# A fused four-layer kernel: three sequences of the first shared experts are moved from their own stage into the head of the fused loop, and scattered rows get a pitch of 1088 bytes

## What is computed

```
scores = softmax(t @ gate_w.T);  weights, indices = top_k(scores, 2)
for e in range(16):
    y = y + swiglu(t, w1[e], w3[e], w2[e]) * weight_of(e)      # routed
z = swiglu(t, sw1, sw3, sw2)                                     # shared: silu(t@sw1.T) * (t@sw3.T) @ sw2.T
return y + z
```

## Time and profile before

| | |
|---|---|
| three runs, median (lowest to highest) | 1965.39 us (1960.8 to 1970.16) |
| the profiled execution's own time | 1962.86 us |
| its span | 1961.1 us |
| TensorE matmul busy | 1831.5 us (93%) |
| VectorE / ScalarE / GpSimd busy | 1264.7 / 763.2 / 422.5 us |
| VectorE, one product of `up` (line 769), mean | 0.419 us |
| VectorE, one tile normalised (line 685), mean | 0.418 us |
| ScalarE, one Silu (line 644) / one copy of 512 columns (649) | 0.382 / 0.586 us |

### The profile page before, as it was taken

The page is one execution under the profiler, slowest core; times in us unless marked ns, Lnnn a source line. Parts: engine busy times, 40 slices in busy tenths (PEclk is TensorE's granted clock), DMA queues, the critical chain, the costliest instruction groups (busy, mean ns, idle before and its releaser), DMA issues.

```text
span 1961.1 us, 33597 instructions
## 1 busy us (share of the span) xinstructions
PE 1831.5 (93%) x9969; PEld 1414.6 (72%) x9987; DVE 1264.7 (64%) x3621; ACT 763.2 (39%) x1479; POOL 422.5 (22%) x708
## 2 busy tenths in 40 slices
PE   5999999979989999667999999999999999999998
PEld 3566666547776666445888888888888888888886
DVE  3677677527432222368778877887787778777843
ACT  1466666543223333234433343334333333433321
POOL 1244334331763444300100110011001100110000
PEclk9899999879998999867999999999999999999999
DMA  9900000001332333252012202220222022112210
GB/s 359 220 6 1 0 0 1 1 1 38 114 108 84 94 94 93 81 199 81 25 63 87 82 16 76 87 81 6 87 85 63 25 86 81 46 46 71 66 49 11
DMA packets 92119, 137.87 MB, mean 70 GB/s; under 512 B 18548, under 2 KB 76148, under 8 KB 91508
## 3 DMA queue, kind: packets, MB, share of 16 engines
q1 hardware_dynamic: 85108, 117.83, 19.0%
q0 software_dynamic: 6912, 18.92, 2.7%
HBM read 98.51 MB, written 38.22 MB: 70 GB/s over the span
## 4 chain that ended last, share of the span: by engine, by line
PE 45%; issue 38%; DVE 9%; POOL 4%; ACT 2%; DMA 1%; another core or an unknown queue 1%; DVEq 0%; SPq 0%; POOLq 0%; ACTq 0%
PE bank L599 6%; PE bank L184 5%; PE bank L1151 4%; PE bank L620 4%; PE bank L1216 3%; PE bank L1109 2%; PE bank L548 2%; PE bank L193 2%; PE bank L1157 2%; PE bank L1244 2%; PE bank L1139 2%; PE bank L559 1%; PE bank L610 1%; PE bank L1202 1%; PE bank L528 1%
## 5 line engine op out<-in xcount | busy, mean ns | idle before, releaser
L184 PE MATMUL bank<-moe_xT,up_w 128*128 128x256 f32 x2304 | 546.1, 380 | 0.0
L184 PEld LDWEIGHTS bank<-moe_xT,up_w 128*128 128x128 f32 x2304 | 438.7, 191 | 60.0
L227 ACT ACTIVATE moe_silu<-bank 128x256 f32<-128x256 f32 x288 | 110.4, 383 | 575.6 <-PE bank L184 572.4
L193 PE MATMUL bank<-down_w,moe_hT 128*128 128x256 f32 x1152 | 304.0, 387 | 3.5 <-ACT moe_y L230 2.1
L193 PEld LDWEIGHTS bank<-down_w,moe_hT 128*128 128x128 f32 x1152 | 207.1, 190 | 37.0 <-issue 6.4
L1390 DVE TENSOR_REDUCE q_slots<-bank 128x4 f32<-128x1024 f32 (+1 forms) x96 | 117.7, 1226 | 82.2 <-PE bank L1151 81.6
L1298 ACT ACTIVATE probs<-bank 128x1024 f32<-128x1024 f32 x96 | 98.1, 1022 | 100.4 <-PE bank L1157 100.4
L599 PE MATMUL bank<-up_w,moe_xT 128*128 x320 | 116.8, 488 | 0.7 <-ACT moe_xT L663 0.6
L794 DVE TENSOR_TENSOR moe_h<-moe_silu,bank 128x176 f32<-128x176 f32 x80 | 27.0, 338 | 138.8 <-issue 86.4
L1151 PE MATMUL bank<-kT,qT 16*128 16x256 f32 (+1 forms) x1024 | 115.3, 353 | 0.2 <-issue 0.2
L294 DVE TENSOR_TENSOR moe_hT<-moe_silu,bank 128x256 f32<-128x256 f32 x256 | 107.7, 421 | 8.8
(11 more groups left out here) (287 smaller groups left out, 3181.5 us busy)
## 6 DMA issues: line engine op xcount, KB each, us to landing
up_w<-comb_rows SPq DMA_DIRECT2D x32, 768.0 KB, 6.0
m<-decay_rows SPq DMA_DIRECT2D x16, 1024.0 KB, 4.9
comb_got<-results SPq DMA_DIRECT2D x16, 768.0 KB, 7.7
moe_rows<-sorted_in SPq DMA_DIRECT2D x80, 128.5 KB
sorted_in<-zero SPq DMA_DIRECT2D x10, 1024.0 KB, 9.5
down_w<-comb_rows SPq DMA_DIRECT2D x16, 512.0 KB, 8.4
up_w<-in_up SPq DMA_DIRECT2D x2, 3168.0 KB, 15.0
up_w<-in_up SPq DMA_DIRECT2D x2, 2304.0 KB, 11.9
```

The source lines that it names most:

```text
L184: last = mm(k.bank[:, UP_BANK + i % 3, half * S:(half + 1) * S], m.w_up[:, c, at + half * m.inter:at + (half + 1) * m.inter], m.xT[:, par, ...
L193: last = mm(k.bank[:, SUM_BANK, j * D:(j + 1) * D], m.hT[:, i % 3, j * P:(j + 1) * P], m.w_down[:, m.expert(i), :], start=(i == 0 and j == ...
L227: nc.scalar.activation(m.silu[:, i % 3, :], k.bank[:, UP_BANK + i % 3, 0:S], ACT.Silu).then_inc(m.silu_ready, 1)
```

## The change

Sequences 13, 14 and 15 leave the shared stage (`EARLY = 13`): it goes through 13 sequences, and the 32 scatters are spread over the 27 places of sequences 4 to 12. The three are computed by new steps `l_norm`, `l_turn`, `l_up`, `l_h`, `l_down` in the head of the fused loop, in buffers that belong to the fourth sublayer, with all transposes, and the result of `l_down`, in bank 7, and with one store buffer. The step `l_h` is VectorE's product, which stands apart from `l_up` there. `decay_in` stands ahead of `gate` now. `l_end`, after the first period, waits for the last of these. The copy of the places and the spare operation ahead of the indirect DMAs are gone, and the rows in `pairs` and `sorted_in` are 272 floats, 1088 bytes, apart; whole rows of 1088 bytes are scattered and 1028 of them fetched. The weights of the shared experts stay where they are while the fourth sublayer's weights are loaded: these take other columns.

```diff
+LINE = 16
+LINED = -(-ROW // LINE) * LINE
+PAIR_ROWS = 2
+EARLY = 13
 def shared_steps(chunks):
+    places = chunks * (EARLY - SCATTERS_FROM)
-    for t in range(B):
+    for t in range(EARLY):
...
-            if t >= SCATTERS_FROM and tile < TILES:
+            place = chunks * (t - SCATTERS_FROM) + c + 1
+            while place > 0 and tile < -(-TILES * place // places):
                 yield "scatter", tile, 0
                 tile += 1
-    yield "down", B - 1, 0
+    yield "down", EARLY - 1, 0
...
 def sparse_vector(k, m, dve):
+    v.memset(m.pairs[:, :, :, ROW:], 0.0)
...
 def sparse_pool(k, m, pool):
-            chain.link(g.tensor_copy(m.place[:, 2 * par:2 * par + 2], cols(m.places, t, 2)))
-            g.tensor_tensor(k.pool_spare[:, 0:1], k.minus_half[:, 0:1], k.minus_half[:, 0:1], ALU.add)
             for j in range(2):
-                at = bass.IndirectOffsetOnAxis(m.place[:, 2 * par + j:2 * par + j + 1], 0)
-                g.indirect_dma_start(m.sorted_in, at, m.pairs[:, par, j, :], None).then_inc(m.scattered[par], 16)
+                at = bass.IndirectOffsetOnAxis(m.places[:, 2 * t + j:2 * t + j + 1], 0)
+                g.indirect_dma_start(m.sorted_in, at, m.pairs[:, row, j, :], None).then_inc(m.scattered[row], 16)
...
+def late_tensor(k, m, pe):
+        if what == "l_turn":
+            pe.wait_ge(s.xn_ready, t + 1)
+            pe.wait_ge(s.y_read, t)
...
+        if what == "l_up":
+            pe.wait_ge(s.xT_ready, m.turns + n + 1)
+            if n > 0:
+                pe.wait_ge(s.h_ready, m.up(t - 1, c) + 1)
...
+        if what == "l_down":
+            pe.wait_ge(s.h_ready, m.up(t + 1, 0))
...
+def late_vector(k, m, dve):
+        if what == "l_h":
+            dve.wait_ge(s.silu_ready, m.up(t, c) + 1)
+            if n > 0:
+                dve.wait_ge(s.y_full, m.turns + n)
...
 def head(self):                       # class Tail
+        a, b, c = range(EARLY, B)
+        yield "c_fetch", 0, 0, 0
+        for what, t, i in (("l_norm", a, 0), ("l_turn", a, 0), ("l_up", a, 0), ("c_sum", 0, 0), ("l_up", a, 1), ("c_sum", 0, 1),
+                           ("l_up", a, 2), ("l_h", a, 0), ("c_norm", 0, 0), ("l_h", a, 1), ("c_fetch", 1, 0),
+                           ("experts", 0, 0), ("norm", 0, 0), ("l_h", a, 2), ("l_norm", b, 0), ("norm", 0, 1),
+                           ("l_down", a, 0), ("turn_x", 0, 0), ("l_turn", b, 0), ("feat", 0, 0), ("l_up", b, 0), ("feat", 0, 1),
+                           ("l_h", b, 0), ("l_up", b, 1), ("bcdt", 0, 0), ("l_h", b, 1), ("l_up", b, 2), ("turn_dt", 0, 0),
+                           ("dt", 0, 0), ("table", 0, 0), ("conv", 0, 0), ("one_plus", 0, 0), ("l_h", b, 2), ("table", 0, 1),
+                           ("dt", 0, 1), ("conv", 0, 1), ("l_norm", c, 0), ("dt", 0, 2), ("table", 0, 2), ("turn_dA", 0, 0), ("decay_out", 0, 0), ("decay_in", 0, 0), ("l_down", b, 0),
+                           ("gate", 0, 0), ("conv", 0, 2), ("l_turn", c, 0), ("gate", 0, 1), ("conv", 0, 3), ("l_up", c, 0),
+                           ("silu", 0, 0), ("l_up", c, 1), ("c_sum", 1, 0), ("l_h", c, 0), ("l_up", c, 2), ("c_sum", 1, 1),
+                           ("l_h", c, 1), ("c_norm", 1, 0), ("turn_c", 0, 0), ("turn_c", 0, 1), ("l_h", c, 2),
+                           ("norm", 1, 0), ("norm", 1, 1), ("turn_x", 1, 0), ("l_down", c, 0), ("xdt", 0, 0)):
...
+        yield from self.period(0, 0)
+        yield "l_end", B, 0, 0
+        yield from self.period(1, 1)
```

More of the change, by code:

```diff
@@ new lines, in late_vector, with step @@
+def late_vector(k, m, dve):
+    s, moe = m.sparse, m.moe
+    def step(what, t, par, c):
+        n = t - EARLY
+        if what == "l_norm":
+            if n > 0:
+                dve.wait_ge(s.xT_full, m.turns + n)
+            for j in range(SEQ_TILES):
+                last = normalised(k, moe.xn[:, j, :], SEQ_TILES * t + j)
+            last.then_inc(s.xn_ready, 1)
+        if what == "l_h":
+            w = s.wide(c)
+            dve.wait_ge(s.silu_ready, m.up(t, c) + 1)
+            if n > 0:
+                dve.wait_ge(s.y_full, m.turns + n)
+            k.nc.vector.tensor_tensor(moe.hT[0:w, c, :], moe.silu[0:w, c, :], k.bank[0:w, UP_BANK + c, S:2 * S],
+                                      ALU.mult).then_inc(s.h_ready, 1)
+    return step
@@ L873, with late_sync, step @@
+def late_sync(k, m, sp):
+    s, moe = m.sparse, m.moe
+    def step(what, t, par, c):
+        if what == "l_down":
+            sp.wait_ge(s.y_read, t + 1)
+            sp.dma_start(s.shared_rows(t), moe.y[:]).then_inc(s.stored[t % 2], 16)
+        if what == "l_end":
+            for stored in s.stored:
+                sp.wait_ge(stored, 16 * B // 2)
+    return step
 HEADS, KV = 16, 4
@@ L2172, in head @@
     def head(self):
-        for what, t, i in (("c_fetch", 0, 0), ("c_sum", 0, 0), ("c_sum", 0, 1), ("c_norm", 0, 0), ("c_fetch", 1, 0),
-                           ("experts", 0, 0)):
-            yield what, t, t % 2, i
-        for what, i in (("norm", 0), ("norm", 1), ("turn_x", 0), ("feat", 0), ("feat", 1), ("bcdt", 0), ("turn_dt", 0), ("dt", 0), ("table", 0),
-                        ("conv", 0), ("one_plus", 0), ("table", 1), ("dt", 1), ("conv", 1), ("dt", 2), ("table", 2),
-                        ("turn_dA", 0), ("decay_out", 0), ("gate", 0), ("conv", 2), ("decay_in", 0), ("gate", 1), ("conv", 3), ("silu", 0)):
-            yield what, 0, 0, i
@@ L2180, in head @@
-        for what, i in (("c_sum", 0), ("c_sum", 1), ("c_norm", 0)):
-            yield what, 1, 1, i
-        for i in (0, 1):
-            yield "turn_c", 0, 0, i
-        for what, i in (("norm", 0), ("norm", 1), ("turn_x", 0)):
-            yield what, 1, 1, i
-        yield "xdt", 0, 0, 0
-        for t in (0, 1):
-            yield from self.period(t, t % 2)
+        a, b, c = range(EARLY, B)
[11 more added lines that the diff above has]
+                           ("norm", 1, 0), ("norm", 1, 1), ("turn_x", 1, 0), ("l_down", c, 0), ("xdt", 0, 0)):
+            yield what, t, t % 2, i
@@ L2306, in program @@
         second = Moe(k, 128, 2.5, up_w, down_w, gate1, [(moe1_loaded, 80)], comb_rows)
-        attention, tail = Attention(k, a, gate0), Tail(k, Combine(k, results), Ssm(k, a), second)
+        attention, tail = Attention(k, a, gate0), Tail(k, Combine(k, results), Ssm(k, a), second, Late(k, first, second))
         layers = [attention, first, tail]
```

134 lines of the change are left out of this document (95 added, 39 removed).

## The result

| | median us (lowest to highest, runs) | ratio to before, 95% interval |
|---|---|---|
| before | 1963.93 (1960.8 to 1970.16, 11) | |
| changed | 1974.85 (1970.66 to 1983.54, 11) | 1.0061 [1.0045, 1.0078] |

The forecast was 1963 us, no change. The profiled execution of the changed kernel took 1983.54 us, 8.7 over its median; where that matters, the second profile of the same kernel (e13) stands beside it.

What follows compares the result with a forecast made beforehand. Bounds: TensorE in the routed blocks, TensorE and GpSimd's scatters in the shared stage, an ordered chain through all engines in the head. Head +15.6 and shared stage -15.3 gave +0.3: 1963 us, no change; 8-in-10 range 1949 to 1975.

Steps and rivals of the forecast that it cites:

- I take 2.70 us: Shared stage: time per scatter tile once copy and spare operation go, between bounds of 2.56 and 2.99 us.
- Gain 15.3 us: Shared stage: first fetch of the routed blocks at 571.9 us, not 587.17; bounds, gains of 6 and 20 us.
- The prediction's own sign: Shared stage: the prediction counts as wrong if scatters pass 2.5 or 2.95 us per tile.
- the same 0.45 us: Shared stage: saving taken from the two-buffer round trip of 5.75 us, giving a second limit of 2.65 us per tile.
- Second rival, order on VectorE: Head: VectorE's order costs +23.6 us, shared stage gains only 12; sum +11.6, 1974.5 us; chance 0.13.
- First rival, idle time hides the late work: Head: late work adds only 5 or 6 us; with 2.56 us per tile, -14.5, 1948 us; chance 0.22.
- Third rival, scatters held by the round trip: Shared stage: scatters get no faster, gain 6 to 9 us, sum +7 to +9, 1971 us; chance 0.15.
- Fourth rival, shorter landing: Shared stage: 1088-byte rows land in 2.5 us, giving 3 to 4 us more, 1959.5 us; chance 0.50 together with the forecast.
- Head: Head of the fused loop: three late sequences delay the chain step by step, first weighting +15.6 us.
- is the place that decides: Head: VectorE waits for the Silu of sequence 15's chunk 0, sums and norms behind it; xdt +14.7 us.
- The clock's bounds: Head: +10.6 us if the clock is full from the second chunk on, +23.6 if half after 860 us.
- From there to 912 the first period is set by VectorE's scans as before: Fused loop after the first weighting: the rest of the first period follows VectorE's scans, nothing added.

Runs made afterwards that it cites:

- e13: The changed kernel run once more, unaltered, on chip D: 1976.5 us, 1.0082 of before.
- e12: The changed kernel with space for four pair buffers allocated but two in use, on chip C: 1962.5 us, 0.9991 of before.
- e5: The kernel before with scatter offsets read straight from the table of places, copy and spare operation still issued, on chip B: 1962.8 us, 1.0002 of before.
- e3: The kernel before without the copy of the place and the spare operation, on chip A: 1970.6 us, 1.0031 of before.
- e7: The kernel before with only the move of three sequences and four pair buffers, on chip B: 1970.0 us, 1.0031 of before.
- e8: The changed kernel with four pair buffers in place of two, on chip B: 1961.2 us, 0.9987 of before.
- e4: The kernel before with rows of 1088 bytes in place of 1028, on chip A: 1963.3 us, 0.9994 of before.
- e9: The changed kernel with four pair buffers and the last late sequence's products later on VectorE in the head, on chip C: 1956.9 us, 0.9973 of before.
- e17: The changed kernel with 4352 bytes per partition allocated between the pair buffers and those behind, on chip E: 1973.4 us, 1.0048 of before.
- e16: The kernel before without copy and spare operation, space for four pair buffers, two used, on chip D: 1966.9 us, 1.003 of before.
- e11: The kernel before with four pair buffers, no copy or spare operation, 1088-byte rows, nothing moved, on chip C: 1950.5 us, 0.9926 of before.
- e1: The kernel before without copy and spare operation and with 1088-byte rows, on chip A: 1969.0 us, 1.0013 of before.

## Why the prediction failed, step by step

- **The step that failed is "I take 2.70 us"** per tile in the shared stage, and with it "Gain 15.3 us". The changed kernel took 3.20 (3.01 in e13), and the stage 150.6 us (144.4) against 150.3. The bound given for it, 2.99, "if the removed operations buy nothing", was too narrow: I left out that they can cost. The prediction's own sign, over 2.95 us per tile, came true. What stood in its place is the late delivery of TensorE's increments to ScalarE, with pauses behind it and the half clock that follows. An estimate from the traces: the four pauses that end at 517.0, 541.5, 565.0 and 584.9 us sum to 13.6 us, and the 12 matmuls behind each take 2.6 us more than at full clock, 10.5 in all. e12 has, behind its first pause, 4.9 us of pauses over 1 us and 1.7 of clock. The difference is 17.5 us, and the two stages differ by 17.3. The first pause, which both have, is no part of it.
- Before has late Silus too (4 in its own profile), and there they cost nothing that can be seen: e5, at the same pace and without one, has the same stage of 150.3 us, and no pause of TensorE in before's passes 1.5 us. That it is GpSimd's longer tile that leaves this room is my reading; e3 fits it, which takes only that away and is slower (ratio 1.0031).
- With e13, the profile of the changed kernel that is at its median, the account of the miss is: shared stage 5.9 us shorter and not 15.3, head 11.7 longer and not 15.6, rest 3.5 longer and not 0.
- Where no increment is late, the step is right in all its parts: e12 has 2.66 us per tile, the first fetch 2.5 us after the last issue (3.1 forecast), a stage 17.0 us shorter than before's (15.3 forecast), on another chip. Its total, 1962.5 us (1963 forecast), agrees by luck: its head is 11.4 us longer and not 15.6, its rest 3.4 and not 0. The trace of before already showed late Silus, and I did not read them; these two begin 2.7 and 3.2 us after the recorded end of their matmuls:

```profile
522.39 0.38 ACT L644 ACTIVATE moe_s_silu<-bank 96x256 f32<-96x256 f32 x1 [2.34 <-PE bank L548]
...
525.32 0.38 ACT L644 ACTIVATE moe_s_silu<-bank 128x256 f32<-128x256 f32 x1 [2.55 <-remote]
```

- A slip in the sum: it takes "the same 0.45 us" out of the buffer's round trip, but the lines before it take out 0.30 (0.60 less 0.30). With 0.30 the second limit is (5.75 - 0.30) / 2 = 2.73 us and not 2.65. e12's 2.66 us speaks for the smaller number.
- **Second rival, order on VectorE:** its 1974.5 us is the measured time, by chance. It wanted +23.6 us in the head, 2.8 us per tile and a second gate that ends after 878 us; measured were +16.4, 3.20 and 873.4 us. **First rival, idle time hides the late work:** no head is less than 11.4 us longer in the order as changed. **Third rival, scatters held by the round trip:** 1971 us, near in number but wrong in its reason: the landings' share of VectorE's waits fell to 22.5 us, and e12 with the same two buffers takes 2.66 us per tile.
- **Fourth rival, shorter landing:** in profiles that can tell, rows of 1028 bytes land in 2.7 us (e5 to e7) and rows of 1088 in 2.4 to 2.5 (e8 to e12). e4 alone gives 0.8 us in the stage and nothing measurable in total.
- **Head:** from the first comb_got operation to the first weighting 60.1 us (59.4 forecast, 43.8 before), VectorE's wait for the Silu of sequence 15 7.12 us (8), TensorE idle ahead of the decay's transposes 8.45 us (8). Delays from comb_got on: c_norm +1.8 (+2.0 forecast), decay +7.0 (+7.3), second gate +8.6 (+10.3), xdt +12.6 (+14.7), first weighting +16.3 (+15.6). That VectorE's wait "is the place that decides" isn't shown; e9 supports it for 1.6 us at least. The head as forecast, 15.6 us, is met only by its longer kind. The clock's bounds were used: in six profiles the head is 11.4 to 11.7 us longer than before, in four 16.4 to 16.6. e12 shows the short kind, where three groups run faster than in the changed kernel: the first up matmuls (6.93 for 8.44 us, granted clock 0.78 for 0.64), the second down group (4.12 for 4.88, 0.64 for 0.54) and the last (2.60 for 4.89, 1.00 for 0.54):

```profile
812.12 6.93 PE bank L920 x24
...
842.91 4.12 PE bank L929 x12
...
862.11 2.60 PE bank L929 x12
```

- "From there to 912 the first period is set by VectorE's scans as before" puts a term at nothing: the rest is 0.9 to 3.6 us longer in every kernel with the move than in before. Kernels without it spread from 1089.7 to 1093.1 themselves, so only the upper end counts. The six short heads have the longest rests (1093.5 to 1094.0 us, the long ones 1091.4 to 1092.5), so part of what a short head saves is given back. Head and rest together take 1156.1 to 1159.8 us with the move in its first order and 1140.5 to 1144.0 without.
- **Routed blocks:** 230.5 to 233.1 us in all profiles, so within 2.1 us of before's 232.6 and unchanged, as forecast.
- The table load shows 1.28 us and no drain behind it: the load begins at 868.87 and the gate at 870.16. The drain of 1.38 us that the Trainium skill states (ScalarE: Activation LUTs, What ACT_TABLE_LOAD costs) did not appear here either.

**Still open:** why increments of TensorE arrive late, and whether it is the chip or something else that a group of runs shares. No kernel has a profile from two chips that are known to be of both kinds; the nearest pair is e12 and e17, one memset apart (158 against 108 ns, long before the first scatter). That taking the two operations off GpSimd costs 5 to 6 us (e3, e16) only on chips with late increments is likely by e11, but e11 has four buffers as well; e3 on B or C, and the changed kernel itself there, would settle it.

## What to carry to other kernels

Read in the trace of before how long after a matmul's end its reader begins; where that distance jumps in a stage, a plan that removes slack there can lose all it gains, and the time then depends on where it runs. Before concluding from one run that an edit cured a stall, run the uncured kernel beside it on the same chip. Moving work from a bound stage into idle time costs what the ordered chain there makes of it (11 to 16 us in the head, 12 to 19 with what follows it, for three sequences worth 10), whereas two more buffers and two operations fewer, with nothing moved, gave the best time: 1950.5 us, 0.9926 of before, on a chip without late increments; it was not run on one that has them.

## What was not expected of the hardware

Silus began up to 6.8 us after the recorded end of their matmuls (e13), in the changed kernel at 516.1, 540.6 and 564.1 us, so some 24 us apart, and inside such an episode TensorE's increments arrived one at a time: in e3 at 503.62, 506.45 and 509.31 us, so 2.8 us apart, where the matmuls behind them ended 2.2 us apart or less. The same executions lack up to 71% of the DMA landing signals (e1: 149 of 512 are there) in their traces, beyond the shared stage too, and some 140 to 200 of the engines' own 5,700 increments; the eight others lack none of these. After the changed kernel's four pauses of 3.2 to 4.1 us in the shared stage the granted clock stood at 0.50, the level of 1.2 GHz, and a group of 12 matmuls took 5.5 us in place of 2.9. It doesn't follow every such pause: in e17 the clock stayed at 1.00 behind one of 3.60 us, from 523.4 to 528.4 us.
